# A perceiver block on one core: the order of matrix products inside a step of the cross attention, and the place of the late key writes

## The chip, the core and the metric

The kernel runs on one core of a Trainium2 chip. A core has a matrix engine (TensorE), three engines for elementwise work (VectorE, ScalarE, GpSimd), and a queue engine (SyncE, SP) that issues DMAs. Each runs its own list of instructions in order, and semaphores tie them together. The metric is the device time of one execution in microseconds (us).

## The reference

The layer takes x (4 batches of 256 tokens, 256 wide) and a context (4 x 4,096 tokens, 192 wide). Cut to what matters:

```
x = x + xattn(layernorm(x), ctx)     # 16 heads of 16; 256 queries against 4,096 keys
x = x + attn(layernorm(x))           # 16 heads, causal, over the 256 tokens
x = x + ffn(layernorm(x))            # slots with top-8 routing
# xattn, per head:
q = query @ Wq + bq;  k = ctx @ Wk + bk;  v = ctx @ Wv + bv
a = softmax(clip(q k^T / sqrt(16), -10000, 10000));  out = (a v) @ Wo + bo
```

All is float32. The cross attention makes 4 x 16 x 256 x 4,096 scores and takes most of the time.

## The kernel before, in words

**Precision.** [...] A head takes 51 rows of the array: even heads rows 0 to 50, odd heads rows 64 to 114.

**Groups, units, steps.** The cross attention runs in NQ = 16 groups q: four heads of one batch. A group has 64 units t; a unit is one head against 256 keys. Four units (one for each head) make a step, so a group has 16 steps. In a step TensorE makes
- the scores of four units (`score_half`, L1806: two products of 256 columns each, one bank of three), which ScalarE turns into exponentials (L1026);
- four maxima products, 512 keys against 128 queries of a head (`max_unit`, L1792, one bank of three), which VectorE reduces (L1218). They run AHEAD = 76 units before the scores, because the softmax shift of a group must be known before its scores: the shift stands on extra rows of the query stack;
- where there is a job, nine products (`passes`, L1752) of a half chunk of the key or value projection of later context, all summed in the bank kps. The first four use the upper 64 rows, the other five the lower, and the fifth waits until the fourth has landed (high_done). Jobs exist in 182 of the 256 steps, in all of groups 0 to 10 and 6 steps of group 11;
- the values of the step before (`values`, L1838: eight products, which the chip runs in two passes each).

**Engines around it.** ScalarE copies the halves of a key chunk out of kps (`k_first_half`, L910) and the first half of a value chunk (L930); VectorE copies the second half (L1294). GpSimd splits keys and context (L694 to L696, L744 to L746). At the start of each group it reads a flag, branches, and releases the group's exponentials (clip_done, L801) if nothing has to be clipped; the values wait for it.

**The next group's shift.** From unit 52 on VectorE makes the shift in small operations, `shift_step` (L1224 to L1246). After the values at the end of step 56 to 59 TensorE turns it (`turn_shift`, L1819) into a score bank; ScalarE copies it onto the query rows (L938), VectorE takes a flag from it (L1251), and the third score unit after it needs that bank. The finish of the group before (`finish`, L1642) stands behind step 4 to 7.

**The head.** The context's first 20 chunks (KLEAD) are projected to keys before the loop; their parts are written to memory and read back as stacks (kst). The SP queue issues these in a written order: `write_k`, `write_q`, `load_block`, `load_q`, `load_parted`. ScalarE's copy of key chunk 20 waits for the write of chunk 18.

## Time and profile before

| | us |
|---|---|
| median of three runs | 1,182.41 (1,172.23 to 1,187.26) |
| profiled execution, own time | 1,177.84 |
| its span | 1,176.1 |
| TensorE busy | 1,066.5 (91%) |
| VectorE busy | 837.3 (71%) |
| ScalarE busy | 709.1 (60%) |
| GpSimd busy | 378.1 (32%) |
| mean granted TensorE clock | 0.958 |

In a timeline, a row gives the start, the time covered, engine, line, operation, output and inputs with their shapes, the number of instructions merged into the row, and in brackets how long the engine was idle before and what released it.

### The profile page before, as it was taken

To read this page: it belongs to the slowest core of one execution; us is meant where nothing else is said; L and a number is where in the kernel's file an instruction comes from. 1 tells how busy PE (TensorE), PEld (TensorE's weight loads), DVE (VectorE), ACT (ScalarE), POOL (GpSimd) and SP (SyncE) were. 2 spreads that over 40 slices of the span, in tenths; PEclk is the share of its full clock that TensorE was granted. 3 is DMA by queue.
4 is the path that set the end of the run, shared out by engine and by line. 5 is a ranking of instruction groups with operands and counts; after the bars stand their busy time and mean duration, and the time that the engine had idled before them with its cause. 6 is when DMAs were issued, how large, how long until landed. Compare 5 with 4: busy or idle time off the path is not lost.

```text
span 1176.1 us, 29344 instructions
## 1 busy us (share of the span) xinstructions
PE 1066.5 (91%) x11489; PEld 695.7 (59%) x11489; DVE 837.3 (71%) x1567; ACT 709.1 (60%) x1366; POOL 378.1 (32%) x437
## 2 busy tenths in 40 slices
PE   7899599999999899999999999999999888978997
PEld 6677365655656565656565565655556454645654
DVE  7567487878788886878787878888877513594553
ACT  2122377777677776777777777777666645404432
POOL 4632444444444453444444443130000000203320
PEclk9899699999999998999999999999998899998999
DMA  7744645555546464546555463433532000000001
GB/s 216 234 150 117 215 143 143 166 151 157 152 127 172 121 187 122 166 128 174 140 166 152 142 164 118 122 88 109 159 86 87 21 28 2 1 1 2 3 1 36
DMA packets 120724, 137.24 MB, mean 117 GB/s; under 512 B 21351, under 2 KB 92906, under 8 KB 120554
## 3 DMA queue, kind: packets, MB, share of 16 engines
q1 hardware_dynamic: 115082, 128.86, 37.6%
q10 hardware_dynamic: 5472, 6.23, 1.9%
q8 instruction: 93, 1.52, 0.6%
q14 instruction: 77, 0.63, 0.2%
HBM read 97.20 MB, written 37.81 MB: 115 GB/s over the span
## 4 chain that ended last, share of the span: by engine, by line
PE 78%; DVE 9%; ACT 4%; SPq 3%; issue 3%; DMA 1%; ACTq 0%; POOLq 0%
PE acc L1838 22%; PE st L1806 16%; PE kps L1752 15%; PE mx L1792 7%; PE misc L1792 4%; DVE mxp L1218 3%; DVE free_k L1485 2%; PE setB L2098 1%; ACT prob L1026 1%; DMA kscr<-o_sb 1%; ACT prob L1113 1%; PE acc L1647 1%; PE mx L1642 1%; PE st L2012 1%; PE mx L1788 1%
## 5 line engine op out<-in xcount | busy, mean ns | idle before, releaser
L1218 DVE TENSOR_REDUCE mxp<-mx 128x1 f32<-128x512 f32 x709 | 465.8, 683 | 126.5 <-PE mx L1792 59.2
L1026 ACT ACTIVATE prob<-st 128x512 f32<-128x512 f32 x704 | 384.0, 600 | 161.5 <-PE st L1806 161.3
L1806 PE MATMUL st<-qst,kst 51*128 51x256 f32 x2048 | 364.9, 325 | 30.5 <-DVE flagf L1251 21.9
L1806 PEld LDWEIGHTS st<-qst,kst 51*128 51x128 f32 x2048 | 251.5, 191 | 163.2 <-issue 75.3
L1218 DVE TENSOR_REDUCE mxp<-misc 128x1 f32<-128x512 f32 x315 | 215.0, 683 | 54.9 <-PE mx L1792 32.6
L1792 PE MATMUL mx<-kst,qst 51*128 51x512 f32 x633 | 226.2, 409 | 0.0
L1026 ACT ACTIVATE xn<-st 128x512 f32<-128x512 f32 x320 | 179.1, 600 | 59.5 <-PE st L1806 59.4
L1838 PE MATMUL acc<-prob,v_raw 128*17 128x256 f32 x2816 | 193.8, 394 | 3.6 <-ACT prob L1026 3.6
L1752 PE MATMUL kps<-ctx_p,w_hi 64*128 64x256 f32 x528 | 124.8, 303 | 19.9 <-ACT kraw L910 9.4
L1752 PE MATMUL kps<-w_hi,ctx_p 64*128 64x256 f32 x564 | 132.5, 298 | 8.4
L1792 PE MATMUL misc<-kst,qst 51*128 51x512 f32 x315 | 128.9, 409 | 0.0
L1752 PEld LDWEIGHTS kps<-ctx_p,w_hi 64*128 64x128 f32 x528 | 95.2, 193 | 43.0 <-PE kps L1752 26.4
L746 POOL TENSOR_TENSOR ctx_p<-ctx,ctx_p 128x512 fp32r<-128x512 f32 x91 | 116.6, 1281 | 7.3
L1752 PEld LDWEIGHTS kps<-w_hi,ctx_p 64*128 64x128 f32 x564 | 98.1, 186 | 32.7 <-PE kps L1752 29.9
L1838 PEld LDWEIGHTS acc<-prob,v_raw 128*17 128x17 f32 x2816 | 65.9, 98 | 68.9 <-issue 11.0
L1792 PEld LDWEIGHTS mx<-kst,qst 51*128 51x128 f32 x633 | 105.8, 192 | 1.4 <-DVE mxp L1218 0.2
L744 POOL CAST ctx_p<-ctx 128x512 fp32r<-128x512 f32 x91 | 55.7, 612 | 135.6 <-PE kps L1752 132.4
L694 POOL CAST kraw<-kraw 128x512 fp32r<-128x512 f32 x50 | 30.5, 611 | 192.9 <-ACT kraw L910 173.5
L1838 PE MATMUL acc<-xn,v_raw 128*17 128x256 f32 x1280 | 90.6, 403 | 0.8 <-ACT prob L1026 0.8
L1752 PE MATMUL kps<-w_lo,ctx_p 64*128 64x256 f32 x282 | 75.3, 281 | 0.0
L1752 PE MATMUL kps<-ctx_p,w_lo 64*128 64x256 f32 x264 | 71.1, 283 | 0.0
L696 POOL TENSOR_TENSOR kraw<-kraw 128x512 f32<-128x512 f32 x50 | 64.1, 1282 | 4.0
(428 smaller groups left out, 1262.5 us busy)
## 6 DMA issues: line engine op xcount, KB each, us to landing
kst<-kscr SPq DMA_DIRECT2D x240, 128.0 KB, 2.5
kscr<-kraw SPq DMA_DIRECT2D x100, 256.0 KB, 2.6
kst<-kscr SPq DMA_DIRECT2D x240, 64.0 KB, 2.5
ctx<-in_ctxT SPq DMA_DIRECT2D x93, 128.0 KB, 2.6
ctx<-in_ctxT SPq DMA_DIRECT2D x184, 64.0 KB, 2.3
low<-lscr SPq DMA_DIRECT2D x16, 512.0 KB
kscr<-prob SPq DMA_DIRECT2D x16, 256.0 KB, 3.5
kscr<-o_sb SPq DMA_DIRECT2D x12, 256.0 KB, 4.0
```

The source lines that it names most:

```text
L694: pool.tensor_copy(first.bitcast(F32R), full).then_inc(k_1, 1)
L696: pool.tensor_tensor(full, full, first, ALU.subtract).then_inc(k_2, 1)
L744: pool.tensor_copy(hi, raw).then_inc(part_step, 1)
L746: pool.tensor_tensor(lo, raw, hi.bitcast(F32), ALU.subtract).then_inc(part_step, 1)
L1026: act.activation(exps(unit_at(n)), st_bank("scores", unit_at(n))[:, :], ACT.Exp).then_inc(exp_done, 1)
L1113: act.activation(pexp[n % 3], setB[:, :, 0:3 * P], ACT.Exp).then_inc(a_exp, 1)
L1218: dve.reduce_max(at, bank_of_max(n)[:, :], AX.X).then_inc(max_red, 1)
L1485: dve.tensor_reduce(amax[:, 2 * b + qt, :, r], bank[:, :, qt * P:(2 * qt + 1) * P], AX.X, ALU.max, negate=True).then_inc(a_max, 1)
L1752: mm = pe.matmul(kps[:, g * CH:(g + 1) * CH], ctx_part[:, col] if m else w_part[:, col], w_part if m else ctx_part, start=(i == 0), stop=( ...
L1792: pe.matmul(bank_of_max(n)[:, :], qst[row, 2 * (q % 3) + j // 2, qt * P:(qt + 1) * P], kst[row, j // 2, at:at + 512], start=True, stop=Tru ...
L1806: mm = pe.matmul(st_bank("scores", n)[:, h * T:(h + 1) * T], kst[row, j // 2, at:at + P], qst[row, 2 * (q % 3) + j // 2, :], start=True, s ...
L1838: mm = pe.matmul(acc[32 * j:32 * j + VW, 0:T], v4[:, q // 4 % 2 * 32 + n, h, :], exps(UQ * q + 4 * (n // 2) + j)[:, n % 2 * T:(n % 2 + 1) ...
```

## The change

1. In a step the products stand in a new order. All four score units of a step are made in it (before, the fourth was made at the start of the next step, side by side with the first of that step). The units come in the order 1, 0, 2, 3 and not 0, 2, 1, 3, and between the fourth and the fifth projection product stand three others.
2. Places that follow from it: the copies of ScalarE and VectorE and the finish's sums one unit later, the turn of the shift behind unit 59; the operations of the shift on VectorE one unit earlier, the first two together.
3. In the head SP writes the late key chunks (16 to 19) before the queries of batches 1 to 3 and the output biases, and loads context chunk 20 before the last two early key blocks. VectorE turns the low column after the low parts of the weights and not before. GpSimd's memset of the second half of the value columns goes from the head to the end of group 1.

```diff
@@ the order of units, and the place of the turned shift
-            return n // 4 * 4 + (0, 2, 1, 3)[n % 4]
+            return n // 4 * 4 + (1, 0, 2, 3)[n % 4]
...
-            if t == 58 and q + 1 < NQ:
+            if t == 59 and q + 1 < NQ:
                 st_users.append(("shift", q + 1))
@@ SP, head
             load_q(1)
+            sp.wait_ge(v_ps, VLEAD)
+            sp.wait_ge(k_ps, 17)
+            load_parted(0, KLEAD)
             for n in range(10, RB):
                 load_block(n)
             load_q(2)
-            write_q(1)
-            sp.wait_ge(v_ps, VLEAD)
-            sp.wait_ge(k_ps, 17)
-            load_parted(0, KLEAD)
...
-            write_q(2)
-            write_q(3)
-            for n, name in enumerate(("L0_xattn_bo", "L0_attn_bo")):
...
             write_k(KLEAD - 1)
+            for b in range(1, B):
+                write_q(b)
+            for n, name in enumerate(("L0_xattn_bo", "L0_attn_bo")):
...
@@ GpSimd
-            pool.wait_ge(qscr_w, 256)
-            pool.memset(v4[:, 32:64, :, DH:VW], 1.0).then_inc(vcol_set, 1)
...
+                if q == 1:
+                    pool.wait_ge(qscr_w, 256)
+                    pool.memset(v4[:, 32:64, :, DH:VW], 1.0).then_inc(vcol_set, 1)
@@ ScalarE: key and value copies
-                if t % 4 == 1:
+                if t % 4 == 2:
@@ VectorE, shift_step: rows' maximum and clip now both at t == 52, the next ones at 53 to 56
-                elif t == 53:
                     dve.wait_ge(m_row, q + 1)
...
@@ VectorE, loop
-                if t % 8 == 5 and v_job(q, t // 8) is not None:
+                if t % 8 == 6 and v_job(q, t // 8) is not None:
-                if t == 6 and q > 0:
+                if t == 7 and q > 0:
@@ TensorE, a step
-                    if n:
-                        score_half(n - 1, 0)
-                    score_half(n, 0)
-                    if n:
-                        score_half(n - 1, 1)
-                    score_half(n, 1)
-                    if n and n - 1 + AHEAD < NU:
-                        max_unit(n - 1 + AHEAD)
                     if more:
                         max_unit(n + AHEAD)
+                    score_half(n + 1, 0)
+                    score_half(n + 1, 1)
+                    score_half(n, 0)
                     next(some, None)
-                    score_half(n + 2, 0)
-                    next(some, None)
-                    score_half(n + 2, 1)
+                    score_half(n, 1)
                     next(some, None)
                     if more:
                         max_unit(n + 1 + AHEAD)
                     next(some, None)
                     next(some, None)
-                    score_half(n + 1, 0)
-                    next(some, None)
-                    score_half(n + 1, 1)
+                    score_half(n + 2, 0)
+                    if more:
+                        max_unit(n + 2 + AHEAD)
+                    score_half(n + 2, 1)
                     next(some, None)
                     if more:
-                        max_unit(n + 2 + AHEAD)
+                        max_unit(n + 3 + AHEAD)
                     next(some, None)
+                    next(some, None)
+                    score_half(n + 3, 0)
+                    next(some, None)
+                    score_half(n + 3, 1)
                     next(some, None)
```

TensorE's list in a step with a key job, before, from the first projection product on (st are scores, mx and misc maxima, kps projection products):

```order
L1752 MATMUL kps<-w_hi,ctx_p 128x256 [waits v_out,part_step]
L1806 MATMUL st<-qst,kst 128x256 [waits exp_done]
L1752 MATMUL kps<-w_hi,ctx_p 128x256
L1806 MATMUL st<-qst,kst 128x256
L1752 MATMUL kps<-w_lo,ctx_p 128x256
L1792 MATMUL mx<-kst,qst 128x512 [waits max_red]
L1752 MATMUL kps<-w_hi,ctx_p 128x256
L1752 MATMUL kps<-w_hi,ctx_p 128x256 [waits high_done]
L1806 MATMUL st<-qst,kst 128x256 [waits exp_done]
L1752 MATMUL kps<-w_hi,ctx_p 128x256
L1806 MATMUL st<-qst,kst 128x256
L1752 MATMUL kps<-w_lo,ctx_p 128x256
```

The same place now, from the second maxima product on:

```order
L1791 MATMUL misc<-kst,qst 128x512 [waits max_red]
L1751 MATMUL kps<-w_lo,ctx_p 128x256
L1751 MATMUL kps<-w_hi,ctx_p 128x256
L1805 MATMUL st<-qst,kst 128x256 [waits exp_done]
L1791 MATMUL mx<-kst,qst 128x512 [waits max_red]
L1805 MATMUL st<-qst,kst 128x256
L1751 MATMUL kps<-w_hi,ctx_p 128x256 [waits high_done]
L1791 MATMUL mx<-kst,qst 128x512 [waits max_red]
L1751 MATMUL kps<-w_hi,ctx_p 128x256
L1751 MATMUL kps<-w_lo,ctx_p 128x256
L1805 MATMUL st<-qst,kst 128x256 [waits exp_done]
L1751 MATMUL kps<-w_hi,ctx_p 128x256
```

The product that waits for high_done followed its releaser directly; now two halves of a score unit and a maxima product stand between, and the fourth maxima product stands behind it.

VectorE's list around the shift, before, from unit 52 on (mxp<-mx and mxp<-misc are the reductions of maxima products):

```order
L1218 TENSOR_REDUCE mxp<-misc 128x1 [waits max_ps,m_row]
L1224 TENSOR_REDUCE rowmax<-mxp 128x8 [waits max_red]
L1218 TENSOR_REDUCE mxp<-mx 128x1 [waits max_ps]
L1228 TENSOR_SCALAR shift<-rowmax 128x8 [waits low_col,m_row]
L1218 TENSOR_REDUCE mxp<-mx 128x1 [waits max_ps]
L1232 TENSOR_REDUCE spad<-shift 128x1 [waits shift_ps,m_clip]
L1234 TENSOR_SCALAR spad<-shift 128x4x2
L1218 TENSOR_REDUCE mxp<-misc 128x1 [waits max_ps]
L1237 SCALAR_TENSOR_TENSOR sres<-shift,spad 128x8 [waits m_1]
L1218 TENSOR_REDUCE mxp<-mx 128x1 [waits max_ps]
L1241 SCALAR_TENSOR_TENSOR spad<-sres 128x4x2 [waits m_res]
L1218 TENSOR_REDUCE mxp<-mx 128x1 [waits max_ps]
```

And now:

```order
L1218 TENSOR_REDUCE mxp<-misc 128x1 [waits max_ps,m_row]
L1224 TENSOR_REDUCE rowmax<-mxp 128x8 [waits max_red]
L1227 TENSOR_SCALAR shift<-rowmax 128x8 [waits low_col,m_row]
L1218 TENSOR_REDUCE mxp<-mx 128x1 [waits max_ps]
L1231 TENSOR_REDUCE spad<-shift 128x1 [waits shift_ps,m_clip]
L1233 TENSOR_SCALAR spad<-shift 128x4x2
L1218 TENSOR_REDUCE mxp<-mx 128x1 [waits max_ps]
L1236 SCALAR_TENSOR_TENSOR sres<-shift,spad 128x8 [waits m_1]
L1218 TENSOR_REDUCE mxp<-misc 128x1 [waits max_ps]
L1240 SCALAR_TENSOR_TENSOR spad<-sres 128x4x2 [waits m_res]
L1218 TENSOR_REDUCE mxp<-mx 128x1 [waits max_ps]
L1245 TENSOR_TENSOR spad<-sres,spad 128x4x2 [waits m_clip,m_2]
```

Each operation behind the first stands one reduction earlier, and the last one (L1245) behind the reduction of unit 56.

SP's list in the head, before, from the halves of context chunks 17 and 18 on (kscr are key writes, qscr query writes, bo the output biases; two more pairs of query writes and the load of context chunk 20 stand right above):

```order
L594 DMA ctx<-in_ctxT 64x256 x2
L493 DMA qscr<-v_raw 256x1x256
L496 DMA qscr<-v_raw 128x256
L493 DMA qscr<-v_raw 256x1x256
L496 DMA qscr<-v_raw 128x256
L493 DMA qscr<-v_raw 256x1x256
L496 DMA qscr<-v_raw 128x256
L493 DMA qscr<-v_raw 256x1x256
L496 DMA qscr<-v_raw 128x256
L598 DMA bo<-in_L_xattn_bo 128x256
L598 DMA bo<-in_L_attn_bo 128x256
L486 DMA kscr<-kraw 256x1x256 x4
```

And now, from the same halves on:

```order
L593 DMA ctx<-in_ctxT 64x256 x2
L486 DMA kscr<-kraw 256x1x256 x4
L486 DMA kscr<-o_sb 256x1x256 x2
L478 DMA ctx<-in_ctxT 128x256
L480 DMA ctx<-in_ctxT 64x256 x2
L486 DMA kscr<-o_sb 256x1x256 x2
L493 DMA qscr<-v_raw 256x1x256
L496 DMA qscr<-v_raw 128x256
```

The key writes moved ahead of six pairs of query writes and of two bias loads.

## Rows read from the trace of the kernel before

**Rows 1.** The page's part 4: shares of the chain that ended last, by engine

```profile
PE 78%; DVE 9%; ACT 4%; SPq 3%; issue 3%; DMA 1%; ACTq 0%; POOLq 0%
```

**Rows 2.** Timeline of TensorE, one step with projection products, columns as described above

```profile
375.10 0.51 PE L1806 MATMUL st<-qst,kst 51*128 51x256 f32 x4
375.44 0.39 PE L1792 MATMUL misc<-kst,qst 51*128 51x512 f32 x1
...
376.02 0.77 PE L1752 MATMUL kps<-w_hi,ctx_p 64*128 64x256 f32 x2
376.41 0.38 PE L1806 MATMUL st<-qst,kst 51*128 51x256 f32 x1
...
376.98 0.28 PE L1752 MATMUL kps<-w_lo,ctx_p 64*128 64x256 f32 x1
377.19 1.06 PE L1838 MATMUL acc<-prob,v_raw 128*17 128x256 f32 x16
378.17 0.51 PE L1806 MATMUL st<-qst,kst 51*128 51x256 f32 x4
```

**Rows 3.** Timeline of VectorE in the same step

```profile
375.86 0.69 DVE L1218 TENSOR_REDUCE mxp<-misc 128x1 f32<-128x512 f32 x1 [0.58 <-PE mx L1792]
376.47 1.28 DVE L1218 TENSOR_REDUCE mxp<-mx 128x1 f32<-128x512 f32 x2
```

**Rows 4.** Timeline of TensorE, a step without projection products

```profile
800.74 0.39 PE L1806 MATMUL st<-qst,kst 51*128 51x256 f32 x2
...
801.35 0.49 PE L1806 MATMUL st<-qst,kst 51*128 51x256 f32 x2
801.68 0.50 PE L1792 MATMUL mx<-kst,qst 51*128 51x512 f32 x1
```

**Rows 5.** Timeline of TensorE at the end of group 3

```profile
346.28 0.40 PE L1819 MATMUL st<-identb,spad 128*32 128x128 bf16 x9 [0.57 <-DVE spad L1246]
346.61 0.50 PE L1806 MATMUL st<-qst,kst 51*128 51x256 f32 x4
...
349.00 0.35 PE L1806 MATMUL st<-qst,kst 51*128 51x256 f32 x1 [1.54 <-DVE flagf L1251]
```

**Rows 6.** Timeline of VectorE at the end of group 3

```profile
341.49 0.21 DVE L1224 TENSOR_REDUCE rowmax<-mxp 128x8 f32<-128x64 f32 x1
...
343.95 0.35 DVE L1237 SCALAR_TENSOR_TENSOR sres<-shift,spad 128x8 f32<-128x8 f32 x1
...
345.50 0.72 DVE L1246 TENSOR_TENSOR spad<-sres,spad 128x8 bf16<-128x8 f32 x1
...
348.58 0.27 DVE L1251 TENSOR_REDUCE flagf<-st 1x1 f32<-1x128 f32 x1
```

**Rows 7.** Windows: five-step borders of groups 3 and 8, sum over 14; one step

```profile
341.59:361.86 20.27, 17.70 (x212) 11.36 (x211) 15.29 (x35) 13.89 (x29) 10.55 (x13) 0.92 0.39 108
...
613.59:632.31 18.72, 16.18 (x212) 10.63 (x211) 15.27 (x35) 13.89 (x29) 9.12 (x12) 1.00 0.41 116
...
sum 277.11, PE 242.58 PEld 153.24 DVE 209.96 ACT 188.78 POOL 107.03; mean PE 17.33 PEld 10.95 DVE 15.00 ACT 13.48 POOL 7.64
...
799.17:802.11 2.94, 2.94 (x30) 1.69 (x29) 2.49 (x5) 2.07 (x5) 0.00 (x0) 1.00 0.46 142
```

**Rows 8.** Timeline of TensorE, values of group 3's first step

```profile
302.75 1.88 PE L1838 MATMUL acc<-prob,v_raw 128*17 128x256 f32 x14 [1.29 <-ACT prob L1026]
```

**Rows 9.** Timeline of GpSimd: addition of a bias, memset of value columns

```profile
297.77 1.29 POOL L712 TENSOR_TENSOR x_sb<-x_sb,bo 128x512 f32<-128x512 f32 x1 [0.31 <-POOL ctx_p L746]
129.65 1.00 POOL L756 MEMSET v_raw<- 128x512 f32 x1 [0.40 <-DMA qscr<-v_raw]
```

**Rows 10.** Timeline of the SP queue in the head

```profile
130.82 1.33 SPq L486 DMA_DIRECT2D kscr<-o_sb  x2
...
140.01 0.35 SPq L550 DMA_DIRECT2D low<-lscr  x1
```

**Rows 11.** Timeline of ScalarE in the head

```profile
136.89 0.47 ACT L910 ACTIVATE kraw<-kps,bk 128x256 f32<-128x256 f32 x1 [10.95 <-DMA kscr<-o_sb]
```

More of the change, by code:

```diff
@@ L353, in build @@
                 mx_users.append(("max", n + AHEAD))
-            if t == 6 and 0 < q < NQ - 1:
+            if t == 7 and 0 < q < NQ - 1:
                 mx_users.append(("finish", q - 1))
@@ L1035, in _ @@
                         v_copy_half(c, 0)
-                if t == 57 and q + 1 < NQ:
+                if t == 58 and q + 1 < NQ:
                     low_bound(q + 1)
-                if t == 58 and q + 1 < NQ:
+                if t == 59 and q + 1 < NQ:
                     shift_rows(q + 1)
@@ L1228, in shift_step @@
                     dve.tensor_scalar(shift[:, :, :], rowmax[:, :, :], CLIP, -CLIP, ALU.min, ALU.max).then_inc(m_clip, 1)
-                elif t == 54:
+                elif t == 53:
                     dve.wait_ge(m_clip, 2 * q + 1)
@@ L1234, in shift_step @@
                     dve.tensor_scalar(sparts[:, :, :, 0], shift[:, :, :], -1.0, None, ALU.mult).then_inc(m_1, 1)
-                elif t == 55:
+                elif t == 54:
                     dve.wait_ge(m_1, q + 1)
@@ L1238, in shift_step @@
                                              ALU.mult, ALU.subtract).then_inc(m_res, 1)
-                elif t == 56:
+                elif t == 55:
                     dve.wait_ge(m_res, q + 1)
@@ L1242, in shift_step @@
                                              ALU.mult, ALU.max).then_inc(m_2, 1)
-                elif t == 57:
+                elif t == 56:
                     dve.wait_ge(m_2, q + 1)
@@ L1351, in _ @@
                 dve.tensor_tensor(lo, raw, hi.bitcast(F32), ALU.subtract).then_inc(weights_set, 1)
+            turn_low(0)
             def add_norm(k, banks):
@@ L1801, in score_half @@
                     st_free(pe, "scores", n)
-                    if t == 0:
+                    if t == unit_at(0):
                         pe.wait_ge(shift_set, 2 * q + 2)
@@ L1987, in _ @@
                         slot_products(at)
-            for h in range(2):
-                score_half(NU - 1, h)
             values(NQ - 1, 15)
```

3 lines of the change are left out of this document (1 added, 2 removed).

## The prediction

> **What bounds the kernel now.** I read the page first, then stretches of 50 us, then single steps. The chain that ended last lies on TensorE for 78% [rows 1], and most of that in the loop over 1,024 units. There the granted clock is 1.00 but for short drops. So the question is what makes a step long. I call the products of a step by what they make: S0 to S3 the scores (two of 256 columns each), M0 to M3 the maxima (512 columns), p0 to p8 the nine projection products (256 columns), V the 16 passes of the values. Even heads sit on the lower rows of the array, odd heads on the upper ones. S and M go to the rows of their head (units 0, 2 lower; 1, 3 upper), p0 to p3 go to the upper rows, p4 to p8 to the lower.
>
> A step with projection products takes 378.17 - 375.10 = 3.07 us [rows 2]. Its two row halves run side by side. One gap stands out: p3 starts at 376.02 and p4 only at 376.41, 0.39 later, because p4 waits until p3 has landed in the bank, and everything behind p4 queues in order. A step without them takes 2.94 [rows 7]. There S1 waits for a bank until 801.35, and M2 for a reduction [rows 4].
>
> At the end of each group of 16 steps stand the waits for the next shift. The turn waits for VectorE until 346.28, and S2 of the next step waits for the flag until 349.00, 1.54 idle [rows 5]. After most of these borders TensorE then runs at 1.2 GHz for a while: five steps around a border take 20.27 us at mean clock 0.92, and only 18.72 in a border at clock 1.00 [rows 7].
>
> **The step in the new order.** M0 S1 S1 S0 p0 S0 p1 M1 p2 p3 S2 M2 S2 p4 M3 p5 p6 S3 p7 S3 p8 V. The column sums on each row half are unchanged. I lay it out with the spacings of rows 2 and 4: 0.12 for 256 columns, 0.23 for 512, 0.11 more behind a wait (801.35 to 801.68 is 0.33 for 512 columns in two halves). M0 and S1 start at 0, S0 at 0.34, M1 and p2 at 0.58, p3 at 0.69, S2 and M2 at 0.81, S2 again at 0.92. p4 could start at 1.04 and may start at 0.69 + 0.39 = 1.08: nearly the whole gap is covered.
>
> But the step gets a **new wait**. There are three maximum banks, so M3 needs that of M0. M0 is a first product of 512 columns behind a pause, 0.50 long [rows 4]; its reduction starts 0.04 after it (375.44 + 0.39 to 375.86) and takes 0.69 [rows 2, 3]; from a VectorE result to TensorE is 0.06 (345.50 + 0.72 to 346.28) [rows 5, 6]. M3 starts at 1.29, not at 1.08. p5 to p8 and S3 are queued behind it. S3 shares M3's rows and follows at 1.63, its second half with p8 at 1.75, V 0.21 later (376.98 to 377.19) at 1.96. Before, V stood at 377.19 - 375.10 = 2.09. **Gain 0.13 per step with projection products**; if M3 did not wait it would be 0.22 (V at 1.87). A step without them has the same chain, M3 1.29, S3 1.63 and 1.75, V 1.96, against 1.95 now: no gain. ScalarE and VectorE are not the limit: reductions follow each other every 0.60 [rows 3], four make 2.4, and a copy of the value chunk after M2 ends before the next step's M0 is ready.
>
> 182 steps carry projection products. Outside the borders these are 11 in each of the first eleven groups and some 5 more: 126 x 0.13 = **16 us**.
>
> **The borders.** A border at full clock takes 18.72: five steps and the waits. Before, beyond its steps: 0.6 idle until the turn, 0.33 for the turn (346.28 to 346.61), and about 1.9 at S2 (it stands 0.58 behind the step's first product elsewhere, 375.10 to the pair after 375.44, and here 349.00 - 346.61 = 2.39) [rows 2, 5], 2.85 in all. After:
> - The VectorE operations for the shift come one unit earlier and the last stands behind M0 of the step before the turn; it ends before V does, so the turn no longer waits. The turn stays: 0.33.
> - They now fall closer together, on units 52 to 55: maximum of rows and clip in a row 0.34, the next pair 0.24, then 0.28 and 0.08 [rows 6], 0.94. VectorE has 3.48 - 2.94 = 0.54 to spare before the next M0. So M0's reduction, and M3 behind it, come 0.40 late.
> - In the step behind the turn, flag's reduction follows one reduction and not two, and S2 stands later. M0's reduction starts at 0.54, flag's at 1.14 and ends at 1.41 (0.27 long), S2 starts 0.15 later (348.85 to 349.00) at 1.56 [rows 5, 6]. From there p4 and M3 at 1.90, V at 2.58 instead of 1.96: 0.6.
> - The finish of a group now comes behind four maxima; VectorE's sums delay the next M0 by 0.13.
>
> That makes 1.46 for 2.85, and five steps x 0.13: 18.72 - 1.39 - 0.65 = 16.68. The 14 borders of groups 0 to 13 took 277.1 [rows 7]; 14 x 16.68 = 233.5. **Gain 43.6 us**, about half of it time at 1.2 GHz which I let go together with the long idle stretches. Borders without projection products gain little of it; the sum holds them too.
>
> I keep a part of the drops. A border in rows 7 shows no drop at the same idle time, so whether one comes is partly a matter of position. I take back 3 us. The Trainium skill (TensorE: Matmul & The Clock Gate, "Why this matters for your kernels") asks for no idle gaps over about 3 us between bursts. By that rule these borders should never have dropped; the trace differs, with a drop behind gaps of 0.6 and 1.5 us.
>
> **Value group 0 behind the border.** V of the first step waits for GpSimd's release, which follows its branch: 302.75, 1.29 idle [rows 8]. That chain (split, addition of a bias 1.29 long [rows 9], branch) starts at a product two steps before and does not get shorter; two steps get shorter by 0.26. In q = 1 to 4, where the addition stands, the wait is then 1.55 each, 6.2 together, and the memset moved there adds its 1.00 [rows 9] in one: **-7 us**. Without the addition it just fits.
>
> **The head.** TensorE stands still behind ScalarE's first key copy, which waits 10.95 until 136.89 for the write of a late key chunk, issued at 130.82 (two, until 132.2) and landed 4.7 later [rows 10, 11]. Six pairs of query writes and two bias loads (about 1.25 a pair and 0.5 a load on this queue, 8.4 together) go behind the late key writes, so that write is out at 122.5 to 123.8 and lands at about 127.5, when the first projection is just done. **Gain 9.4.** The SP queue pays later: it issued the low row's read at 140.01 [rows 10] and does so now at 139, while the loop is 10 us ahead. The first key block of the loop stands right behind that read, so it leaves at 139.1 and lands by 143 (0.8 to issue the half that M needs and 2.6, the page's median to land); M0 of the sixth step wants it at 140.5. I take 2.8 off: **+7 us** (4 to 11). VectorE's low weight parts now stand ahead of the turn of the low column, 0.1. The last step's scores no longer spill into an extra piece: **+1 us**.
>
> **Sum.** 16 + 44 - 3 - 7 + 7 + 1 = 58. The profiled execution took 1,177.8 us, so **1,120**. The three other runs had a median of 1,182 (1,172 to 1,187); I forecast from the profiled one.
>
> **Rivals.**
> - *The clock drops stay* (0.17). The drop follows any pause at a border, and now V of q = 1 to 4 adds four. For it: the border at q = 2 dropped twice over. Against: the idle time at a border halves. Price: 14 drops x 1.5 us: 1,140.
> - *M3's wait is milder* (0.08), as by the 0.22 per step: 0.09 x 182 = 16 us more: 1,104.
> - *The order gives nothing back* (0.10): M3's wait takes the whole 0.39, the flag's wait only moves, and only the head gains. Then 1,170. It would need M3 at 1.42 or later; VectorE would have to be busy when M0 lands, and it is idle there [rows 3].
> - *Products on the same rows do not follow closely* (0.05, slower). In the new step four neighbours share their rows (S1 S1, p2 p3, S2 p4, p5 p6) where one did. If each exposed its weight load, 0.11 (what a wait exposes) to 0.19, three would cost 0.33 to 0.57 in 182 steps: 60 to 104 us against a gain of 58. At 0.19 the time is 1,224; it decides from 0.11 on. Against it: two halves of S2, on the same rows, start 0.11 apart (800.74, 0.39 for two of 0.28) with nothing between [rows 4]. The same page of the Trainium skill ("The mechanism" under packing small matmuls) says that a weight load overlaps matmuls in flight only when the rows differ; that speaks against this order, and rows 4 do not bear it out.
>
> **How the numbers follow.** Forecast 0.60 at 1,120, its own range 1,108 to 1,134 (head 4 to 11, drops 0 to all but the long ones, step 0.09 to 0.17). With the milder wait below and the staying drops above I get 1,098 to 1,152, which leaves out 0.1 to 0.2. A measurement tells 2% (24 us) from no change here: faster is under 1,158. The forecast and the first two rivals are there: 0.85; the third, within 2%: 0.10; the last: 0.05.
>
> **What would show it.** Steps 2.94 long in all groups, M3 starting some 1.29 behind M0 with a VectorE reduction as releaser, p4 no longer waiting 0.39 behind p3; borders near 16.7 at clock 1.00; the first key copy at 127 with TensorE going on at once; a short wait for a key block near 140; V of q = 1 to 4 waiting 1.5. The prediction is wrong if steps stay at 3.07, if borders keep a clock of 0.92, or if the flag still costs over a microsecond.

## The result, and the profile after

| | before | changed |
|---|---|---|
| median, us (runs) | 1,179.45 (1,172.23 to 1,187.26; 4) | 1,130.61 (1,122.78 to 1,133.68; 4) |
| ratio, 95% interval | | 0.9575 (0.9491 to 0.9659) |
| profiled execution, its span | 1,177.84, 1,176.1 | 1,133.68, 1,131.9 |
| mean granted TensorE clock | 0.958 | 0.969 |

The changed kernel is 4.2% faster. Run again on another chip (below) it had a median of 1,125.94 and a ratio of 0.9566 (0.9534 to 0.9598). The forecast was 1,120, and 1,098 to 1,152 the range. Two slow executions, one of 1,198.73 of the kernel before and one of 1,869.4 of the version with the new head alone (below), are left out of all ratios.

Part 4 of the page, the chain that ended last, as in [rows 1]. TensorE's share fell, VectorE's rose:

```profile
PE 74%; DVE 15%; ACT 5%; issue 4%; DMA 1%; SPq 1%; ACTq 0%; POOLq 0%; DVEq 0%
```

A step with projection products, TensorE's timeline (for [rows 2]):

```profile
509.49 0.50 PE L1791 MATMUL misc<-kst,qst 51*128 51x512 f32 x1
...
510.07 0.28 PE L1751 MATMUL kps<-w_lo,ctx_p 64*128 64x256 f32 x1
510.19 0.28 PE L1751 MATMUL kps<-w_hi,ctx_p 64*128 64x256 f32 x1
...
510.55 0.39 PE L1751 MATMUL kps<-w_hi,ctx_p 64*128 64x256 f32 x1
510.77 0.50 PE L1791 MATMUL misc<-kst,qst 51*128 51x512 f32 x1
...
511.45 1.06 PE L1837 MATMUL acc<-prob,v_raw 128*17 128x256 f32 x16
512.44 0.50 PE L1791 MATMUL mx<-kst,qst 51*128 51x512 f32 x1
```

VectorE in the same step (for [rows 3]):

```profile
510.02 0.69 DVE L1218 TENSOR_REDUCE mxp<-misc 128x1 f32<-128x512 f32 x1 [0.46 <-PE misc L1791]
```

This is the forecast step. M0 starts at 509.49; p3 (510.19) follows p2 on the same rows 0.12 behind; p4 starts 1.06 behind M0 (forecast 1.08); M3 1.28 (1.29), 0.06 after M0's reduction ends (510.02 + 0.69); the values 1.96 (1.96). The step takes 512.44 - 509.49 = 2.95, and 2.93 to 2.95 in all groups; only the one ahead of the border takes 3.01.

The five-step borders, windows view (for [rows 7]; groups 3, 8 and 13, and the sum of 14):

```profile
329.40:347.88 18.48, 15.79 (x212) 11.11 (x210) 15.30 (x34) 13.81 (x29) 10.08 (x12) 1.00 0.46 127
...
581.71:598.87 17.16, 15.72 (x213) 11.06 (x211) 15.36 (x34) 13.82 (x29) 9.10 (x11) 1.00 0.37 109
...
826.94:842.95 16.01, 14.98 (x166) 9.51 (x166) 13.93 (x33) 12.18 (x25) 0.00 (x0) 1.00 0.44 123
sum 246.80, PE 221.00 PEld 151.88 DVE 210.51 ACT 187.62 POOL 107.66; mean PE 15.79 PEld 10.85 DVE 15.04 ACT 13.40 POOL 7.69
```

Twelve of the 14 have clock 1.00. The sum is 30.3 less than 277.1.

At the end of group 3 (for [rows 5, 6]), TensorE, then VectorE, then GpSimd:

```profile
331.43 0.50 PE L1791 MATMUL mx<-kst,qst 51*128 51x512 f32 x1
...
332.79 0.49 PE L1791 MATMUL misc<-kst,qst 51*128 51x512 f32 x1 [0.86 <-DVE mxp L1218]
...
334.34 0.41 PE L1818 MATMUL st<-identb,spad 128*32 128x128 bf16 x9
334.67 0.50 PE L1791 MATMUL mx<-kst,qst 51*128 51x512 f32 x1
...
336.24 0.35 PE L1805 MATMUL st<-qst,kst 51*128 51x256 f32 x1 [0.59 <-DVE flagf L1250]
```

```profile
330.26 0.52 DVE L1236 SCALAR_TENSOR_TENSOR sres<-shift,spad 128x8 f32<-128x8 f32 x1
...
331.30 0.87 DVE L1240 SCALAR_TENSOR_TENSOR spad<-sres 128x8 bf16<-128x8 f32 x1
332.06 0.68 DVE L1218 TENSOR_REDUCE mxp<-misc 128x1 f32<-128x512 f32 x1
```

```profile
330.14 0.61 POOL L693 CAST kraw<-kraw 128x512 fp32r<-128x512 f32 x1 [4.45 <-ACT kraw L910]
330.83 1.28 POOL L695 TENSOR_TENSOR kraw<-kraw 128x512 f32<-128x512 f32 x1
```

The turn (334.34) no longer waits, and the flag costs 0.59 of idle time for 1.54. But in the step before the turn M3 waits 0.86: L1236 and L1240 of VectorE last 0.52 and 0.87, and each ends within 0.06 of the end of the GpSimd operation beside it (330.14 + 0.61 = 330.75 and 330.83 + 1.28 = 332.11). These two are the split of a key chunk, a cast and the subtraction of its result.

In the head (for [rows 10, 11]), the SP queue, then TensorE's weight loads:

```profile
135.96 1.34 SPq L543 DMA_DIRECT2D lscr<-lowr  x4
140.47 0.35 SPq L550 DMA_DIRECT2D low<-lscr  x1
140.92 0.36 SPq L452 DMA_DIRECT2D kst<-kscr  x1
...
143.04 0.43 SPq L454 DMA_DIRECT2D kst<-kscr  x1
```

```profile
147.55 0.28 PEld L1791 LDWEIGHTS misc<-kst,qst 51*128 51x128 f32 x1 [4.45 <-DMA kst<-kscr]
```

The wait of 10.95 for the key write is gone, and one of 4.45 for a key block is there. The block is four transfers, issued from 140.92 to 143.04, and TensorE waits for all four; the last landed 4.5 after its issue, at 147.5. The granted clock fell to 0.5 during this wait, from 146.3 to 153.2.

At the start of the last group TensorE runs at half clock; its timeline, then a window around it:

```profile
888.21 1.91 PE L1837 MATMUL acc<-prob,v_raw 128*17 128x256 f32 x16 [1.87 <-ACT prob L1026]
```

```profile
887.00:909.00 22.00, 19.84 (x136) 11.16 (x136) 3.05 (x9) 5.29 (x11) 0.00 (x0) 0.53 0.11 37
```

Sixteen passes take 1.91 there and 1.06 in the step above. The granted clock is 0.5 from 887.0 to 907.5.

**Where the time went, in every kernel.** Worked out from the start of the values in each step, us: up to the values of the sixth step of group 0 (**head**); the other steps of groups 0 to 13 outside the borders (**steps**, 150 of them); the 14 **borders**; the rest of **group 14**; the first three steps of the last group (**15a**); its rest (**15b**); and the **tail**. The kernels below row two are those of the experiments.

| profiled execution | head | steps | borders | 14 | 15a | 15b | tail | span |
|---|---|---|---|---|---|---|---|---|
| before | 156.7 | 456.3 | 277.1 | 48.2 | 15.7 | 38.7 | 183.2 | 1,176.1 |
| changed | 154.7 | 441.4 | 246.8 | 45.3 | 21.0 | 37.6 | 185.1 | 1,131.9 |
| changed, again | 153.7 | 441.6 | 243.1 | 46.0 | 17.2 | 37.6 | 182.2 | 1,121.4 |
| order only | 152.4 | 441.6 | 242.5 | 45.1 | 21.0 | 37.6 | 182.2 | 1,122.5 |
| order only, again | 156.0 | 441.1 | 245.9 | 45.1 | 21.1 | 37.6 | 182.3 | 1,129.1 |
| head only | 150.1 | 456.6 | 280.1 | 47.7 | 15.9 | 38.7 | 183.2 | 1,172.4 |
| p4 behind p3 | 152.3 | 457.5 | 245.4 | 45.3 | 17.8 | 37.6 | 181.1 | 1,137.0 |
| half reduction | 148.7 | 420.8 | 225.8 | 42.3 | 17.2 | 37.6 | 182.3 | 1,074.7 |
| M3 late | 151.0 | 431.7 | 242.0 | 46.6 | 17.8 | 37.6 | 181.1 | 1,107.8 |
| block first | 145.6 | 441.3 | 245.7 | 45.0 | 14.4 | 37.6 | 184.4 | 1,114.0 |
| bias inside | 154.2 | 441.5 | 238.1 | 46.5 | 15.8 | 37.6 | 181.2 | 1,115.0 |
| split later | 153.6 | 441.6 | 235.0 | 46.4 | 15.8 | 37.6 | 181.1 | 1,111.1 |
| clearing later | 154.1 | 441.3 | 245.5 | 45.5 | 17.3 | 37.6 | 183.2 | 1,124.6 |
| all five | 146.3 | 431.8 | 223.0 | 42.8 | 12.9 | 37.6 | 183.8 | 1,078.1 |

"Steps" repeats within 0.6 between equal orders. With the new order "15a" follows the clock: 12.9 with none of it at half clock, 14.4 with 3.4 us, 17.2 to 17.8 with 10 to 12 us, 21.0 to 21.1 with 19 to 20 us.

### The profile page after: what moved, and what is told of

It is laid out like the page before. It is cut to its first block, busy times and chain, and to the rows that moved or that the text cites. A ratio compares the mean times of both kernels' runs of the same rounds, so it can differ in the third digit from the quotient of the medians.

```text
span 1131.9 us, 29343 instructions
## 1 busy us (share of the span) xinstructions
PE 1045.3 (92%) x11489; PEld 716.1 (63%) x11489; DVE 841.4 (74%) x1567; ACT 704.3 (62%) x1366; POOL 378.2 (33%) x437
## 4 chain that ended last, share of the span: by engine, by line
PE 74%; DVE 15%; ACT 5%; issue 4%; DMA 1%; SPq 1%; ACTq 0%; POOLq 0%; DVEq 0%
PE acc L1837 21%; PE st L1805 12%; PE mx L1791 11%; PE kps L1751 8%; DVE mxp L1218 7%; PE misc L1791 5%; DVE free_k L1484 2%; ACT prob L1026 2%; PE st L1646 2%; PE mx L1787 2%; PE setB L2093 1%; PE acc L1646 1%; ACT prob L1113 1%; PE mx L1641 1%; PE st L2007 1%
## 5 line engine op out<-in xcount | busy, mean ns | idle before, releaser
L1026 ACT ACTIVATE prob<-st 128x512 f32<-128x512 f32 x704 | 374.2, 598 | 142.3 <-PE st L1805 141.6
L1805 PE MATMUL st<-qst,kst 51*128 51x256 f32 x2048 | 393.7, 297 | 16.7 <-DVE flagf L1250 8.1
L1805 PEld LDWEIGHTS st<-qst,kst 51*128 51x128 f32 x2048 | 308.7, 189 | 39.0 <-ACT prob L1026 13.2
L1791 PE MATMUL mx<-kst,qst 51*128 51x512 f32 x633 | 273.6, 456 | 9.5 <-DVE mxp L1218 6.6
L1026 ACT ACTIVATE xn<-st 128x512 f32<-128x512 f32 x320 | 170.6, 597 | 55.4 <-PE st L1805 55.0
L1791 PEld LDWEIGHTS mx<-kst,qst 51*128 51x128 f32 x633 | 116.8, 187 | 87.9 <-issue 58.0
L1791 PE MATMUL misc<-kst,qst 51*128 51x512 f32 x315 | 143.4, 455 | 8.8 <-DMA kst<-kscr 4.0
L1751 PE MATMUL kps<-w_hi,ctx_p 64*128 64x256 f32 x564 | 138.5, 307 | 0.0
L1751 PE MATMUL kps<-ctx_p,w_hi 64*128 64x256 f32 x528 | 132.7, 317 | 3.4 <-DVE w_lo L1348 3.4
L1791 PEld LDWEIGHTS misc<-kst,qst 51*128 51x128 f32 x315 | 58.7, 186 | 47.2 <-issue 27.9
```

The source lines that it names most:

```text
L1026: act.activation(exps(unit_at(n)), st_bank("scores", unit_at(n))[:, :], ACT.Exp).then_inc(exp_done, 1)
L1751: mm = pe.matmul(kps[:, g * CH:(g + 1) * CH], ctx_part[:, col] if m else w_part[:, col], w_part if m else ctx_part, start=(i == 0), stop=( ...
L1791: pe.matmul(bank_of_max(n)[:, :], qst[row, 2 * (q % 3) + j // 2, qt * P:(qt + 1) * P], kst[row, j // 2, at:at + 512], start=True, stop=Tru ...
L1805: mm = pe.matmul(st_bank("scores", n)[:, h * T:(h + 1) * T], kst[row, j // 2, at:at + P], qst[row, 2 * (q % 3) + j // 2, :], start=True, s ...
```

## The experiments

All ratios are to the kernel before on the same chip, with 95% intervals. The changed kernel's is 0.9575, and 0.9566 again. The times that were expected started mostly from its profiled execution (1,133.68), the slowest of its four, so many measured times lie below both ranges; there the traces decide between the theories.

**The two parts of the change apart.** The first has the head of before and the loop of the change, the second the reverse.

> The changed kernel with the head as it was before: SP's list, the place of the turn of the low column and GpSimd's memset are undone; the loop is the new one. Theory A (the loop makes nearly all of the difference, the head's 8.5 us are mostly given back at the first key block of the loop): values of the first step at 140 to 141 as before, no idle time of 4 us for a key block near 143, values of step 4 at about 153, time 1,134 to 1,139. Theory B (the forecast's sum, head worth 7): 1,141 or more. In both, steps stay at 2.94.

Measured: 1,122.36 (1,118.85 to 1,127.33), ratio 0.9526 (0.9462 to 0.9591), below Theory A's range too. TensorE did not wait for a key block, and the first values came at 136.2, not at 140 to 141; in the repeat below they came at 140.1, so the head differs by 4 us between executions of one program.

> The kernel before with only the new head (SP's list, turn of the low column, memset at the end of group 1); the loop is the old one. Theory A: values of the first step near 132 instead of 140.6, then an idle time of 4 to 5 us of TensorE for a key block near 145, and half clock behind it; in all 0 to 3 us less than before, 1,175 to 1,178. The memset in group 1 shows as 1 us at that border. Theory B (the forecast): 7 us less, 1,171. Steps stay at 3.07.

Measured: 1,178.09 (nine of ten from 1,170.53 to 1,181.60, the tenth 1,869.4), ratio 0.9975 (0.9938 to 1.0012), no difference that can be told. The order alone makes the whole gain. With the old order the new head reaches the sixth step 6.6 earlier in the profiled execution (150.1 for 156.7), of which the span keeps 3.7: the borders took 3.0 more. The edit touches only that of group 1, by its memset, and it took 20.52 for 20.27; the rest of the 3.0 is where the clock fell. Here the key block landed at 145.09, just as TensorE came to it; in the changed kernel TensorE came to it at 143.6, and it landed at 147.5. With the new order nothing was left of the 6.6, so the question came up whether the head's part even costs.

**The same two versions again, side by side.**

> The changed kernel as it is, a second time, beside the version with the new order alone. Theory A: the head's part of the change brings nothing once the new order is in: TensorE starts its values 4 us earlier, and then stands still 4 us for a key block that the SP queue issues at 140.9 behind the query writes. From the traces the fifth values of group 0 stand at 154.7 here and at 152.4 with the old head: 2 us slower, ratio of this kernel to the order alone 1.000 to 1.006. The 20 us at 1.2 GHz at the start of the last group (its first three steps 21.0 us) are a matter of position and need not come back: 1,120 to 1,131. Theory B: the head's part gains as it does with the old order (156.7 to 150.1): then this kernel is the faster of the two by 3 to 6.

> The new order alone with the old head, a second time, on the same chip as the changed kernel. Theory A: 1,118 to 1,126, level with the changed kernel or up to 7 us below it. Theory B: 3 to 6 above it.

Measured: 1,125.94 (1,123.19 to 1,130.19) and 1,125.72 (1,117.35 to 1,132.59), ratios 0.9566 (0.9534 to 0.9598) and 0.9549 (0.9507 to 0.9590). Theory A: with the new order the head's part is worth nothing. The sixth step stands at 153.7 and 154.7 with it, at 152.4 and 156.0 without. The wait for the key block is in both executions with the new head and in neither without it; here it is in the second:

```profile
146.35 0.28 PEld L1791 LDWEIGHTS misc<-kst,qst 51*128 51x128 f32 x1 [5.57 <-DMA kst<-kscr]
```

**The fifth projection product back behind the fourth.** This undoes the one piece of the order that covers the 0.39.

```diff
                     next(some, None)
+                    next(some, None)
                     score_half(n + 2, 0)
                     if more:
                         max_unit(n + 2 + AHEAD)
                     score_half(n + 2, 1)
-                    next(some, None)
```

> The changed kernel with the fifth projection product moved back right behind the fourth (p0 S0 p1 M1 p2 p3 p4 S2 M2 S2 M3 p5 ...); the rest of the new order stays. Theory A (the gain of a step comes from covering the landing of the fourth product): p4 starts 0.39 behind p3 again with nothing under way, steps with projection products take 3.05 to 3.10, those without stay at 2.94; 182 steps x 0.13 make 23 us more than the changed kernel, 1,152 to 1,158. Theory B (the gain comes from making whole steps, not from this gap): steps stay at 2.94 and the time at 1,131 to 1,135.

Measured: 1,138.56 (1,137.68 to 1,145.68), ratio 0.9682 (0.9617 to 0.9747). Between the two ranges; the trace decides:

```profile
515.44 0.75 PE L1751 MATMUL kps<-w_hi,ctx_p 64*128 64x256 f32 x2
515.81 0.50 PE L1791 MATMUL mx<-kst,qst 51*128 51x512 f32 x1
...
516.82 0.62 PE L1837 MATMUL acc<-prob,v_raw 128*17 128x256 f32 x8
```

M0 stood at 514.74, so the values start 2.08 behind it, and the step is 3.07 again. "Steps" goes from 441.4 to 457.5: 16.1, and 456.3 is before's. The borders keep their gain (245.4). So the covered wait is worth 16, and the borders' 30 come with the other placements; which of these brings how much, no run separates.

**Half a reduction for M0.** VectorE reduces 256 of the 512 columns of the first maxima product of each step, so that half of the keys are left out of that maximum.

```diff
-                dve.reduce_max(at, bank_of_max(n)[:, :], AX.X).then_inc(max_red, 1)
+                cols = slice(0, 256) if n >= AHEAD and n % 4 == 0 else slice(0, 512)
+                dve.reduce_max(at, bank_of_max(n)[:, cols], AX.X).then_inc(max_red, 1)
```

> The changed kernel in which VectorE reduces only 256 of the 512 columns of the first maxima product of each step of the loop (this leaves half of the keys out of that maximum). Theory A (the fourth maxima product waits for the first one's reduction, and everything behind it queues): the reduction is 0.27 shorter, the wait is gone, steps with projection products take 2.85 to 2.87 and those without 2.83 to 2.86 (each 0.08 to 0.1 less), in all 18 to 24 us less than the changed kernel: 1,109 to 1,116. Theory B (ScalarE or the projection handoff sets the step): steps stay at 2.94, time at 1,128 to 1,134.

Measured: 1,079.63 (1,076.46 to 1,083.24), ratio 0.9175 (0.9116 to 0.9234), far more than Theory A named.

```profile
484.43 0.50 PE L1792 MATMUL misc<-kst,qst 51*128 51x512 f32 x1
484.65 0.27 PE L1752 MATMUL kps<-w_hi,ctx_p 64*128 64x256 f32 x1
...
485.21 1.06 PE L1838 MATMUL acc<-prob,v_raw 128*17 128x256 f32 x16
```

M0 stood at 483.37: M3 now follows at 1.06 with p4, the values at 1.84, and the step is 2.83. In a step without projection products, where nothing else limits, it is 2.66 for 2.93. So M3's wait for M0's reduction costs up to 0.11 in the one and 0.27 in the other; up to, because the edit also takes 0.27 of work a step off VectorE. The step before the turn fell from 4.06 to 2.84. There, in group 3, L1237 and L1241 (L1236 and L1240 above) last 0.17 and 0.19: the first starts 0.04 ahead of GpSimd's cast, the second between the cast and the subtraction, and only the last shift operation, which has time, meets the subtraction (0.96 for 0.18).

**The fourth maxima product behind the last scores.** It lets M3 be late without anything queued behind it but p8.

```diff
-                    if more:
-                        max_unit(n + 3 + AHEAD)
-                    next(some, None)
                     next(some, None)
                     score_half(n + 3, 0)
                     next(some, None)
                     score_half(n + 3, 1)
                     next(some, None)
+                    if more:
+                        max_unit(n + 3 + AHEAD)
+                    next(some, None)
```

> The changed kernel with the fourth maxima product of a step three projection products later: p4 p5 S3 p6 S3 p7 M3 p8 instead of p4 M3 p5 p6 S3 p7 S3 p8. Nothing is left out. Theory A (as for the half reduction): M3 starts at 1.5 to 1.6 behind the step's first product, when the first one's reduction has long landed, p5 to p8 and S3 no longer queue behind a wait, steps take 2.84 to 2.90, the time falls by 10 to 25 us to 1,106 to 1,121. Theory B: M3's 512 columns now stand at the end of the step with nothing beside them and put the values off by as much as the wait did: steps at 2.92 to 2.98, time unchanged.

Measured: 1,113.50 (1,109.61 to 1,116.34), ratio 0.9448 (0.9398 to 0.9498).

```profile
499.01 0.39 PE L1805 MATMUL st<-qst,kst 51*128 51x256 f32 x1
...
499.35 0.39 PE L1791 MATMUL misc<-kst,qst 51*128 51x512 f32 x1
499.43 0.28 PE L1751 MATMUL kps<-w_lo,ctx_p 64*128 64x256 f32 x1
499.68 1.06 PE L1837 MATMUL acc<-prob,v_raw 128*17 128x256 f32 x16
```

M0 was at 497.78. S3 starts 1.23 behind it (1.63 in the changed kernel), the values at 1.90, and the step is 2.86 to 2.89 in all groups, 0.06 less with nothing taken off VectorE: "steps" 9.7 less. This is the forecast's new wait, seen from the other side.

**The head: the first key block ahead of the low row.** SP issues the block before the write and read of the low row and the two bias loads.

```diff
-            for n, name in enumerate(("L0_xattn_bo", "L0_attn_bo")):
...
-            write_low(0)
-            read_low(0)
             for q in range(NQ):
...
                         load_block(8 * q + k + RB)
+                    if q == 0 and k == 0:
+                        write_low(0)
+                        read_low(0)
+                        ...
```

> The changed kernel in which SP issues the first key block of the loop before it writes and reads the low row of group 0 and the output biases. Theory A (TensorE's idle time near 143 is the SP queue's backlog, above all the 3 us that it waits for the low row to land): the block is issued near 135.5 and lands by 139, TensorE does not wait for it, values of step 4 at about 144 instead of 150.6, no half clock behind it; 5 to 8 us less than the changed kernel, 1,123 to 1,127. Theory B (the transfers themselves are crowded): the wait moves to the next block, 0 to 2 us less.

Measured: 1,116.29 (1,114.16 to 1,121.76), ratio 0.9474 (0.9421 to 0.9528). The block is issued 7.6 earlier than 140.92:

```profile
133.29 0.39 SPq L452 DMA_DIRECT2D kst<-kscr  x1
...
135.14 1.33 SPq L543 DMA_DIRECT2D lscr<-lowr  x4
138.04 0.35 SPq L550 DMA_DIRECT2D low<-lscr  x1
```

The sixth step stands at 145.6, 9.1 earlier than in the changed kernel and 11.1 earlier than before. Against the two executions with the old head and the new order (152.4 and 156.0) it is 6.8 and 10.4. That is what the late key writes can bring once the queue behind them is mended; the same edit with the old head was not run.

**GpSimd's bias additions and memset inside the group.** They stand in the middle of the group and not at its end, ahead of the next flag, in both branches; the second one is that in which nothing is clipped.

```diff
-                if q == 1:
-                    ...
-                if 1 <= q <= 4:
-                    ...
+            # the same statements, called aside(q)
...
                         if t % 8 == 7:
                             ctx_split(q, t // 8 + 2)
+                        if t == 31:
+                            aside(q)
...
                             k_split(k_job(q, k))
                         ctx_split(q, k + 2)
+                        if k == 3:
+                            aside(q)
```

> The changed kernel in which GpSimd adds the output bias (groups 1 to 4) and makes the memset of the value columns (group 1) in the middle of a group and not at its end. Theory A (values of a group's first step wait for GpSimd's release, whose chain these operations lengthen): the idle 1.3 to 2.0 us before the first values of groups 2 to 5 goes, and with it the half clock that follows two of them; borders of groups 1 to 4 come down to those of groups 6 to 9; 7 to 10 us less, 1,121 to 1,125. Theory B (the branch itself is the wait): under 2 us less.

Measured: 1,117.99 (1,116.31 to 1,120.38), ratio 0.9483 (0.9436 to 0.9530). The values of the first step of groups 2 to 5 waited 2.0, 1.4, 1.3 and 1.6 us more than a step in the changed kernel, and 0.1 to 0.5 here; the borders sum to 238.1 for 246.8, of which some 2 to 3 are two drops of the clock that are missing too.

**GpSimd's split of a group's last key chunk behind the shift.** One wait more on GpSimd, for VectorE's last shift operation. (It is the group's seventh job and its fourth key chunk; the expectation for all five calls it the sixth.)

```diff
                         if k % 2 == 0 and k_job(q, k) is not None:
+                            if k == 6 and q + 1 < NQ:
+                                pool.wait_ge(m_3, q + 2)
                             k_split(k_job(q, k))
```

> The changed kernel in which GpSimd splits the key chunk of the group's seventh job only after VectorE's last operation for the next shift. Theory A (in the step before the turn, 4.06 long with projection products against 3.0 without, small VectorE operations take 0.87 and 0.52 instead of 0.18 and 0.35 because GpSimd's subtraction runs at the same time): they take 0.2 to 0.35, the step before the turn takes 3.0 to 3.4, 11 borders x 0.7 to 1.0 make 7 to 11 us less, 1,120 to 1,125. Theory B (that step waits for the projection's copies, not for VectorE): it stays at 4.06.

Measured: 1,113.44 (1,109.36 to 1,118.92), ratio 0.9445 (0.9388 to 0.9502). VectorE in group 3, and GpSimd:

```profile
327.06 0.16 DVE L1238 SCALAR_TENSOR_TENSOR sres<-shift,spad 128x8 f32<-128x8 f32 x1
...
327.74 0.18 DVE L1242 SCALAR_TENSOR_TENSOR spad<-sres 128x8 bf16<-128x8 f32 x1
```

```profile
329.42 1.27 POOL L695 TENSOR_TENSOR kraw<-kraw 128x512 f32<-128x512 f32 x1
```

The same two operations last 0.16 and 0.18, not 0.52 and 0.87, and the step before the turn is 3.01 in all groups and not 4.06. Borders sum to 235.0: 11.8 less, 11 x 1.05 = 11.6. So the delay is the meeting of the two engines, not the shift operations themselves, nor their crowding. The Trainium skill (SBUF — State Buffer, "Who interferes with whom") states that a VectorE instruction with two inputs in SBUF and a GpSimd instruction that reads SBUF exclude each other, and that the later one waits until the other has ended. The trace agrees: both VectorE operations ended 0.03 and 0.06 after GpSimd's, and the reductions beside them, with one input from a bank, kept 0.68.

The same meeting was in the kernel before. There VectorE's last shift operation, on which the turn waits, took 0.72 in rows 6 and ended at 346.22; GpSimd's, a context split, ended at 346.17:

```profile
344.90 1.27 POOL L746 TENSOR_TENSOR ctx_p<-ctx,ctx_p 128x512 fp32r<-128x512 f32 x1
```

It took 0.72 to 0.74 at the borders of groups 0 to 9 and 0.18 at the later ones, and the turn waited 0.57 to 0.59 at these ten and nowhere else. So that wait was of this kind too, and the change took this operation out of it. The two operations ahead of it met GpSimd for 0.19 before (0.35 for 0.16, rows 6), and now meet it for 0.36 and 0.69, together the 1.05.

**The clearing of a buffer behind the last release.**

```diff
-                if q == NQ - 2:
-                    pool.wait_ge(pv_done, 16 * (NQ - 1))
-                    pool.memset(low_vh[:, 0:2048], 0.0).then_inc(sel_set, 1)
+            pool.wait_ge(pv_done, 16 * (NQ - 1))
+            pool.memset(low_vh[:, 0:2048], 0.0).then_inc(sel_set, 1)
```

> GpSimd's clearing of a buffer (128x2048, 1.81 us) stands in the step before the last group's first values ahead of GpSimd's release of value group 0; here it stands behind the loop. Theory A: the values' wait of 1.87 us at 888.21 is this clearing, and the idle time is what puts the last group at 1.2 GHz for 20.5 us (its first three steps 7.63, 6.05 and 7.30 us, where at full clock they take 4.6, 5.2 and 4.7). Then the wait is under 0.2, and the three steps sum to 14.5 to 16: 1.8 + 5 off, ratio to the changed kernel 0.993 to 0.995 (1,122 to 1,126 where that takes 1,131). Theory B: the low clock there follows the waits between products of the last steps of the group before, as the one at 876.2 did in the kernel before; then the wait goes but the clock stays low for 10 to 20 us: 1,127 to 1,130. Theory C: the wait is for something else that the release follows (the branch on the last flag): 1,131.

Measured: 1,122.04 (1,119.56 to 1,126.36), ratio 0.9496 (0.9453 to 0.9539).

```profile
882.36 1.91 PE L1835 MATMUL acc<-xn,v_raw 128*17 128x256 f32 x16
...
886.40 1.91 PE L1835 MATMUL acc<-prob,v_raw 128*17 128x256 f32 x16
```

The wait is gone (the row at 886.40 has no bracket), but in this execution the half clock came all the same, and came earlier, from 879.9 on: Theory B for the clock. The median, though, lies at the edge of Theory A's range, and the profiled execution was the slowest of its four; whether the edit shortens the half clock on average is open. The 17.3 of 15a is no less than the repeat of the changed kernel has without the edit (17.2). Over the kernels with the new order, half clock near the start of the last group took 20.5, 17.1 to 10.2, 3.4 or 0 us, and began up to 11.7 before or 5.7 after its first values. What sets it was not found.

**All five edits together.**

> Five edits to the changed kernel at once, that were or are run alone: the fourth maximum behind the last score product; the first key block on the SP queue ahead of the low row; the bias additions and one memset of GpSimd in the middle of the group; GpSimd's split of the sixth key chunk behind VectorE's shift operations; the clearing of a buffer behind the last release. Theory A: they act at different places and add. From the traces: steps 2.88 for 2.94, 0.06 x 170 = 10; the key block 7; release waits of groups 1 to 4, 6; the step before the turn back from 4.06 to about 2.95 in eleven groups, 12 (of these 1 or 2 are already in the first); the last group 2 to 7. Sum 35 to 40 from 1,132 of the profiled execution: 1,092 to 1,097, first values of group 15 at about 845. Theory B: with the step before the turn short again, the turn waits for VectorE's shift (as in the kernel before, 0.6 each) or the release of value group 0 is late in more groups, and the gains of the borders halve: 1,102 to 1,108. Theory C: the shorter borders bring back drops of the clock: over 1,108.

Measured: 1,085.43 (1,080.11 to 1,088.22), ratio 0.9193 (0.9159 to 0.9228). Windows of group 3, and the sum of 14; then the start of the last group:

```profile
309.08:325.17 16.09, 15.33 (x213) 10.93 (x211) 14.33 (x34) 13.45 (x29) 8.64 (x11) 1.00 0.54 162
...
sum 223.03, PE 213.83 PEld 147.16 DVE 199.44 ACT 183.46 POOL 98.13; mean PE 15.27 PEld 10.51 DVE 14.25 ACT 13.10 POOL 7.01
```

```profile
842.00:857.00 15.00, 13.22 (x158) 7.93 (x154) 2.96 (x9) 8.17 (x17) 1.81 (x1) 1.00 0.26 88
```

It is the fastest version: 8.1% under the kernel before and 4% under the change. The gain of the profiled execution over that of the changed kernel is 53.8 of span: the fastest of six against the slowest of four. By the ratios it is some 45 (0.9575 - 0.9193 = 0.038 of 1,180). Both are more than the 35 to 40 of Theory A. By part, of the 53.8: head 8.4, steps 9.6, borders 23.8, group 14 2.5, 15a 8.1, tail 1.4. In the borders that is the sum of the single edits (11.8, 8.7, and 3 to 5 of "M3 late"); what the expectation left out is the clock, which stays at full speed from 135 to 946 in this execution. Theory B's wait did not come: the step of the turn takes 3.86, as with "M3 late" alone.

## Why the prediction was right

The time fell in the range and near the forecast, and the forecast's own range (1,108 to 1,134) held all ten runs of the changed kernel. The profiled executions give 1,177.84 - 1,133.68 = 44 for 58, and that execution was the slowest of its four; the repeat (1,123.19) gives 55, and the medians of the table at the top give 49. The mechanism was as forecast, but for what is named below as mis-sized or left out. All four parts came out below the sum (steps by 1, borders by 4, the head by 5, the end by 4), so it is not errors that cancel which keep the time near the forecast. By term, in the profiled executions:

- **Steps, 16: right.** 14.9 measured, 16.1 when undone. M3 at 1.28, p4 at 1.06, the values at 1.96 behind M0, and steps without projection products unchanged. That the step ahead of each border takes 3.01 was not in it.
- **M3's new wait: right.** The price was put at 0.09 a step; half a reduction gave back 0.11, M3 at a later place 0.06.
- **Borders, 44 - 3 - 7 = 34: 30.3.** Of these some 18 are the borders themselves (18.72 to 17.17 ten times, 17.91 to 17.15, 16.6 to 16.0 three times, each read from borders without a drop or a release wait), where the sum had 21; the other 12 are drops that went, less release waits that came. This split is an estimate. The waits for GpSimd (some 7 over groups 0 to 4) and the drops (two left of nine) were as forecast. The turn's and the flag's step took 3.77 for the 3.87 that the sum holds, and the finish 3.47 for 3.59: its 0.13 more did not come. **Mis-sized:** the step before the turn. It was given 0.40 for VectorE's crowded shift operations and took 1.12 (4.06 for 2.94). The spacings of 0.28 and 0.08 came from rows 6; one unit earlier both operations meet the split of a key chunk, for 0.36 and 0.69, and take 0.44 and 0.76 (330.26 to 330.70, 331.30 to 332.06). Rows 6 had the sign of it: the 0.72 and the 0.35 there are such meetings too, where the same operations last 0.18 and 0.16 without. A border with projection products took 17.2 for 16.68, 6 in eleven; the three without took 16.0, which gives 2 back.
- **Clock drops: right, the cause not shown.** Nine borders before had a drop, two now, and the rival "the drops stay" is out. That it is the shorter idle stretches that keep the clock is argued: the borders of groups 4 and 8 before had the same idle stretches and no drop.
- **Head, 7 (4 to 11): 2.0, and 0 by the medians. Mis-sized.** The first values came 8.5 earlier, as forecast (9.4). The block was put at 139.1, landing by 143; it was issued from 140.92 on and landed at 147.5. The 5.0 between the sum's 142.5 and that are three parts: 1.8 from the later issue, 1.3 because M0 waits for all four transfers (2.1 to issue) and not for half of them (0.8), and 1.9 because the last one took 4.5 to land. The key blocks of that stretch took 3.5 in the median, where I took 2.6 (the page before has 2.5 for key blocks), and the first of them stood behind the read of the low row (512 KB). M0 heads the new step, so all products stand behind it: 4.0 idle where the sum had 2.8, though TensorE itself came to it 3.1 later than the sum's 140.5. The clock fell during that wait, which the sum left out; the values of the sixth step came some 2.3 later by it (an estimate: 3.1 from M0 to the next values for 1.96, then a step of 4.07 for 2.94).
- **The end, 1: -3.2.** The start of the last group was not in the sum. It ran at half clock for 20.5 us, and cost 5.3 more than before; the repeat lost 1.5 there.
- **Products on the same rows: no cost.** p2 and p3 (510.07 and 510.19) follow 0.12 apart, and the step takes what the sum had without such a cost. The slower rival is out. The rule of the Trainium skill that I weighed with it (TensorE: Matmul & The Clock Gate, "The mechanism"), that a weight load overlaps matmuls in flight only when the rows differ, is not borne out by these products.

So the two halves of the change are of unequal worth: the order carries all of it, the head's part nothing until the queue behind it is changed as well.

## What to carry to other kernels

When products are reordered so that a wait is covered, list for each bank who reads the product that last held it, and count that reader's time from the new place; here it gave the new step to 0.01 us. When small operations of VectorE are moved, look at what GpSimd does at the new time, and take their durations from a row with the same neighbour; a duration that varies between groups (0.72 and 0.18 for one operation here) is a sign that there is one. When a transfer is issued earlier in a queue, the next one that anybody waits for is the one to price, with all transfers that its semaphore counts, and with its landing time from that stretch and not from the page's median.

## What the runs showed of the hardware

- A VectorE operation on 128x8 elements with two inputs lasted 0.87 beside a GpSimd subtraction and 0.18 without it; reductions beside the same subtraction stayed at 0.68.
- TensorE fell to 1.2 GHz at the start of the last group in all but one of the kernels with the new order, for 3.4 to 20.5 us, near idle stretches of under 2 us, and also in a kernel where the longest of these had been removed. Two executions of the same program had 13.6 and 20.5 us of it.
- The fifth projection product starts 0.36 behind the fourth with three products between (510.19 to 510.55), and 0.37 with none (515.44 to 515.81; the second of the two lasts 0.38 of the row's 0.75): the wait stays as long, the order only fills it.
